# Score and projection matmuls on column tiles of 32, in a convolution-gate and attention kernel

## The chip, the cores and the metric

One NeuronCore of a Trainium2 chip runs the whole program in one launch. The metric is the device time of one execution in microseconds (us); the time before is the median of three runs.

## What is computed

`x` has 32 images of 64 channels and 16 x 16 pixels. The first layer gates it, the second is a group norm and an attention with 4 heads of 16 channels over the 256 pixels of an image.

```
y  = conv1d(mean(x, pixels), w_c);  yc = sigmoid(x * y)
sa = sigmoid(conv2d([mean_c(yc), max_c(yc)], w_s));  x1 = yc * sa + x
xn = groupnorm(x1, 32 groups) * gn_w + gn_b
q, k, v = split(qkv_w @ xn + qkv_b)         # 4 heads of 16
attn = softmax(q^T k / 4);  out = x1 + proj_w @ (attn v) + proj_b
```

## The kernel before

Two images make a pair, with the 64 channels of each on 64 of the 128 partitions; there are 16 pairs. A pair has 8 units, one for each image and head, and a unit has a score matrix of 256 x 256.

A unit's scores are computed twice. First `s(u)` (L663, matmul L670) makes q^T k into a bank of PSUM (the accumulator memory), and DVE takes the negated row maximum from it (L540). Then `st(u)` (L674, matmul L682) makes the transposed scores k^T q with one more contraction row, which holds that maximum, and ACT takes the exponential (L400). q and k are fp32 values split into bf16 parts; six products of parts are stacked into 96 contraction rows (`KQ`), so a score matmul is 96 or 97 rows by 128 columns of weights, with 256 moving columns, and a unit needs two of them for S and two for ST. Each has two banks, so `s(u)` waits for the reduction of unit u-2 (`max_done`) and `st(u)` for the exponential of unit u-2 (`exp_done`). `pv` (L686, matmul L696) multiplies the exponentials by v in fp32, each head on 32 columns of its own; an fp32 matmul runs as two passes, and each pass has a record of its own. `proj` (L718, matmul L726) is the output projection in fp32, on 64 columns for each image. `qk` (L707), `v` (L715) and `groupstats` (L734) are fp32 matmuls with 128 columns of weights. `maxt` (L741) transposes the maxima of a pair onto 16 rows.

The work is a pipeline of turns, its order written out by hand for each engine. Turn k does S of pair k+1, ST of pair k (its second half of slots) and of pair k-1 (its first half), PV of pair k-1 and the projection of pair k-2. A turn has 8 slots u. PE's order in it is: S, ST, maxt, qk(1) | S, ST, v | S, ST, pv | S, ST, pv | S, ST, proj | S, ST, pv | S, ST, pv | S, ST, groupstats, qk(0). Turns 2 to 9 are a loop of two laps with four turns in its body; the others are written out. Turns -1 and 0 also have `keep_busy` matmuls (L586), which do no work for the result.

The split parts of q and k go to HBM and come back stacked: SP writes `parts_dram` (L263), and one turn later reads it with six transfers (L255 and L256) into `qs` and `ks` for pair k+2. On SP's queue these six stand behind the transfer of the maxima of pair k (L243), which waits for ACT's copy `maxrow` (L388) of `maxt`'s result:

```
wait(sp, mrow_ready, k + 1)
sp.dma_start(qs[KQ:KQ + 1, slot(0), ...], maxrow[:, slot(0), :]).then_inc(mrow_in, 16)
...
wait(sp, parts_out, 16 * (k + 3))
```

The first S of a turn waits for all six (`stack_in`).

Of the kernel before, what the change touches and what calls it, by code (L numbers as in the profile page):

```python
# [22 lines left out]
P = 128  # L23
IMAGES, C, SIDE = 32, 64, 16
N = SIDE * SIDE
# [7 lines left out]
KQ = SLOTS * HD  # L33
# [18 lines left out]
def program(nc, x, w_rows, vecs, w_all, select, consts, out):  # L52
    ctx = ExitStack()
    with ctx:
        def sb(name, shape, dt=F32):
            return ctx.enter_context(nc.sbuf_tensor(name, shape, dt))
# [46 lines left out]
        qs = sb("qs", [P, RING, HEADS, 2, N], BF16)  # L103
        ks = sb("ks", [P, RING, HEADS, 2, N], BF16)
# [9 lines left out]
        onorm = sb("onorm", [P, 2 * N])  # L114
# [5 lines left out]
        w_p = wall[:, 384:448]  # L120
# [3 lines left out]
        s_bank = [bank[0], bank[1]]  # L124
        st_bank = [bank[2], bank[3]]
# [4 lines left out]
        y_psum = bank[7][:, 0:256]  # L130
# [34 lines left out]
        def wait(eng, semaphore, value):  # L165

            if not isinstance(value, int) or value > 0:
                eng.wait_ge(semaphore, value)
# [12 lines left out]
        def stands_in(aside, k, u):  # L181

            if isinstance(k, int) and (k, u) in aside:
                aside[k, u]()
# [397 lines left out]
        def _(pe):  # L582
# [70 lines left out]
            for a in range(2):  # L653
                mm = pe.matmul(bank[5][64 * a:64 * a + 64, 0:1], w_p, b_v, start=True, stop=True)
# [7 lines left out]
            def turn(k, slot, has, lap):  # L662
                def s(u):  # L663

                    a, h = u // HEADS, u % HEADS
                    wait(pe, max_done, UNITS * (k + 1) + u - 1)
                    if u == 0:
                        wait(pe, stack_in[slot(1)], lap(1) * 96)
                    for t in range(TILES):
                        mm = pe.matmul(s_bank[u % 2][:, t * N:(t + 1) * N], qs[0:KQ, slot(1), h, a, t * P:(t + 1) * P],  # L670
                                       ks[0:KQ, slot(1), h, a, :], start=True, stop=True)
                    mm.then_inc(s_ready, 1)

                def st(u):  # L674

                    d, unit = (-1, u + LEAD) if u < LEAD else (0, u - LEAD)
                    a, h = unit // HEADS, unit % HEADS
                    wait(pe, exp_done, UNITS * k + u - LEAD - 1)
                    if unit == 0:
                        wait(pe, mrow_in, 16 * (k + 1))  # L680
                    for t in range(TILES):
                        mm = pe.matmul(st_bank[u % 2][:, t * N:(t + 1) * N], ks[0:KQ + 1, slot(d), h, a, t * P:(t + 1) * P],  # L682
                                       qs[0:KQ + 1, slot(d), h, a, :], start=True, stop=True)
                    mm.then_inc(st_ready, 1)

                def pv(a, t):  # L686

                    if t == 0:
                        wait(pe, exp_done, UNITS * (k - 1) + HEADS * (a + 1))
                        if a == 1 and isinstance(k, int) and k == PAIRS:  # L690
                            pe.wait_ge(norm_step, 4 * (k - 1) + 1)
                        if a == 0:
                            wait(pe, norm_step, 4 * (k - 2) + 1)
                            wait(pe, vs_ready, k)
                    for h in range(HEADS):
                        mm = pe.matmul(o_bank[32 * h:32 * h + 32, a * N:(a + 1) * N], vs[:, slot(-1), t, a, h, :],  # L696
                                       pt[:, HEADS * a + h, t, :], start=(t == 0), stop=(t == TILES - 1))
                    if t == TILES - 1:
                        mm.then_inc(pv_done, 1)

                def qk(a):

                    d = 4 - a
                    if a == 0:
                        wait(pe, xn_ready, k + 5)
                        wait(pe, z32_ready, k + 4)
                    mm = pe.matmul(z_bank[:, a * N:(a + 1) * N], w_qk[a], xn[:, slot(d), :], start=True, stop=True)  # L707
                    if a == 1:
                        mm.then_inc(z_ready, 1)

                def v():

                    wait(pe, mrow_ready, k + 1)
                    for t in range(TILES):
                        mm = pe.matmul(v_psum[:, t * P:(t + 1) * P], xn[:, slot(1), t * P:(t + 1) * P], w_v, start=True, stop=True)  # L715
                    mm.then_inc(v_ready, 1)

                def proj():  # L718

                    wait(pe, norm_step, 4 * PAIRS + 4 if isinstance(k, int) and k == PAIRS + 1 else 4 * (k - 1))  # L720
                    if has(4):
                        wait(pe, gn_var, k + 5)
                    else:
                        wait(pe, yo_ready, k - 2)
                    for a in range(2):
                        mm = pe.matmul(y_psum[64 * a:64 * a + 64, :], w_p, onorm[:, a * N:(a + 1) * N], start=True, stop=True)  # L726
                    mm.then_inc(y_ready, 1)

                def groupstats():

                    wait(pe, gn_stat, 3 * (k + 6))
                    wait(pe, gn_var, k + 5)
                    wait(pe, yo_ready, k - 1)
                    mm = pe.matmul(gs_psum, groupavg, mv[:, :], start=True, stop=True)  # L734
                    mm.then_inc(gs_ready, 1)

                def maxt():

                    wait(pe, max_done, UNITS * (k + 1))
                    wait(pe, vs_ready, k + 1)  # L740
                    mm = pe.transpose(mt_psum, negmax[:, slot(0), :, :, :].rearrange("p h a t -> p (h a t)"), identb[:, :])  # L741
                    mm.then_inc(mt_ready, 1)

                for u in range(UNITS):
                    stands_in(aside, k, u)
                    if has(1):
                        s(u)
                    if has(-1 if u < LEAD else 0):
                        st(u)
                    if u == 0 and has(0):  # L750
                        maxt()
                    if u == 0 and has(3):
                        qk(1)
                    if u == 1 and has(1):
                        v()
                    if u in (2, 3) and has(-1):
                        pv(0, u - 2)
                    if u == 4 and has(-2):
                        proj()
                    if u in (5, 6) and has(-1):  # L760
                        pv(1, u - 5)
                    if u == 7 and has(5):
                        groupstats()
                    if u == 7 and has(4):
                        qk(0)
# [55 lines left out]
```

## Time and profile before

| what | value |
|---|---|
| median of 3 runs | 203.35 us (202.46 to 203.69) |
| span of the profiled execution | 198.1 us |
| PE busy | 175.1 us, 88%, 1422 matmul records |
| DVE busy | 150.4 us, 76% |
| ACT busy | 122.6 us, 62% |
| POOL busy | 106.3 us, 54% |
| chain that ended last | PE 55%, DMA 16%, SP's queue 12%, DVE 7% |

The profiled execution has no time of its own beside its span: the span runs from its first to its last instruction, and the runs' median lies 5.2 us above it. PE is TensorE's matmuls, PEld its weight loads, SPq SyncE's queue of transfers. Busy time overlaps between engines, so the shares don't add up to the span.

### The profile page before, as it was taken

How to read it: one execution, taken by the hardware profiler on the slowest of the kernel's cores; microseconds unless marked ns; L12 is line 12 of the kernel's file. 1: busy time of each engine (PE TensorE's matmuls, PEld its weight loads, DVE VectorE, ACT ScalarE, POOL GpSimd, SP SyncE). 2: the span in 40 equal slices, each digit the busy share in tenths (PEclk: the TensorE clock that was granted, in tenths of full speed). 3: DMA queues.
4: the chain of work that ended last, by engine and by line, in shares of the span. 5: the costliest groups of instructions: out<-in, count | busy, mean ns of one | idle time of the engine just before them, and what ended most of it. 6: DMA issues, size and time to landing. Idle time of an engine off the chain costs nothing.

```text
span 198.1 us, 4537 instructions
## 1 busy us (share of the span) xinstructions
PE 175.1 (88%) x1422; PEld 95.9 (48%) x1422; DVE 150.4 (76%) x327; ACT 122.6 (62%) x250; POOL 106.3 (54%) x181
## 2 busy tenths in 40 slices
PE   7579869796859899989999999999999998988981
PEld 2156557363535456454645556464655644453320
DVE  0867696477847898978889898988998779697263
ACT  3075323261538587858777787877868786666860
POOL 4991562665737476848595776759556360101110
PEclk9999996999999999999999999999999999999999
DMA  3930405599696663837474665847475573800001
GB/s 81 361 102 18 109 2 149 112 243 187 168 197 161 146 147 122 164 108 164 154 192 113 175 116 150 160 124 185 132 200 108 165 155 112 187 2 26 4 26 53
DMA packets 19558, 26.16 MB, mean 132 GB/s; under 512 B 3757, under 2 KB 16469, under 8 KB 19541
## 3 DMA queue, kind: packets, MB, share of 16 engines
q1 hardware_dynamic: 18960, 25.40, 51.9%
q10 hardware_dynamic: 580, 0.55, 1.2%
q8 instruction: 9, 0.15, 0.3%
q14 instruction: 9, 0.07, 0.1%
HBM read 17.29 MB, written 8.42 MB: 130 GB/s over the span
## 4 chain that ended last, share of the span: by engine, by line
PE 55%; DMA 16%; SPq 12%; DVE 7%; issue 4%; POOL 4%; ACT 1%; POOLq 0%; DVEq 0%
PE bank L696 14%; PE bank L670 12%; PE bank L682 10%; DMA ks<-parts_dram 8%; PE bank L707 7%; DMA parts_dram<-parts 6%; SPq L255 5%; SPq L256 4%; PE bank L726 4%; PE bank L715 2%; DMA con<-consts 2%; DVE maps L453 1%; PE bank L609 1%; POOL tapprod L289 1%; SPq L209 1%
## 5 line engine op out<-in xcount | busy, mean ns | idle before, releaser
L540 DVE TENSOR_REDUCE negmax<-bank 128x2 bf16<-128x512 f32 x128 | 86.9, 681 | 25.2 <-PE bank L670 24.8
L400 ACT ACTIVATE pt<-bank 128x512 f32<-128x512 f32 x128 | 75.4, 596 | 21.9 <-PE bank L682 21.7
L670 PE MATMUL bank<-ks,qs 96*128 96x256 bf16 x256 | 49.7, 275 | 7.4 <-DMA ks<-parts_dram 6.3
L682 PE MATMUL bank<-qs,ks 97*128 97x256 bf16 x256 | 48.8, 272 | 1.7 <-ACT pt L400 1.0
L696 PE MATMUL bank<-pt,vs 128*32 128x256 f32 x512 | 40.7, 391 | 0.1
L670 PEld LDWEIGHTS bank<-ks,qs 96*128 96x128 bf16 x256 | 18.4, 97 | 44.9 <-issue 26.4
L682 PEld LDWEIGHTS bank<-qs,ks 97*128 97x128 bf16 x256 | 23.9, 98 | 8.7 <-ACT pt L400 3.3
L339 POOL TENSOR_TENSOR xall<-yo,xall 128x256 f32 (+1 forms) x15 | 10.9, 729 | 26.8 <-ACT yo L420 26.8
L325 POOL TENSOR_TENSOR rest<-z,parts 128x512 f32<-128x512 f32 x15 | 17.4, 1158 | 14.2 <-ACT z L409 10.7
L707 PE MATMUL bank<-xn,wall 128*128 128x256 f32 x64 | 22.2, 436 | 0.0
L311 POOL TENSOR_TENSOR sq<-gmv 128x1 f32<-128x1 f32 x16 | 3.1, 193 | 34.4 <-DVE gmv L501 34.4
L586 PE MATMUL bank<-warm 128*128 128x512 bf16 x60 | 18.8, 427 | 1.4 <-POOL warm L280 1.4
L335 POOL TENSOR_TENSOR parts<-rest,parts 128x512 bf16<-128x512 f32 x15 | 17.4, 1157 | 1.3
L696 PEld LDWEIGHTS bank<-pt,vs 128*32 128x32 f32 x512 | 10.3, 108 | 13.7 <-issue 11.6
L392 ACT ACTIVATE xn<-xall,gnb,gna 128x256 f32<-128x256 f32 (+1 forms) x16 | 9.5, 592 | 11.6 <-DVE gnb L507 11.6
L521 DVE STREAM_TRANSPOSE otok<-bank 128x512 f32<-128x512 f32 (+1 forms) x17 | 11.5, 676 | 5.0 <-PE bank L696 5.0
L406 ACT ACTIVATE parts<-bank,vec 128x512 bf16<-128x512 f32 x16 | 10.9, 682 | 7.0 <-PE bank L707 7.0
L388 ACT COPY maxrow<-bank 16x128 bf16<-16x128 bf16 x16 | 4.1, 254 | 16.9 <-PE bank L741 16.9
L726 PE MATMUL bank<-onorm,wall 128*64 128x256 f32 x64 | 10.4, 405 | 1.6 <-DVE onorm L532 1.6
L532 DVE STREAM_TRANSPOSE onorm<-otok 128x512 f32<-128x512 f32 (+1 forms) x17 | 11.4, 673 | 0.1
L409 ACT ACTIVATE z<-bank,vec 128x512 f32<-128x512 f32 x16 | 11.0, 686 | 0.0
L707 PEld LDWEIGHTS bank<-xn,wall 128*128 128x128 f32 x64 | 10.3, 199 | 1.2
(67 smaller groups left out, 212.2 us busy)
## 6 DMA issues: line engine op xcount, KB each, us to landing
parts_dram<-parts SPq DMA_DIRECT2D x16, 384.0 KB, 2.7
qs<-parts_dram SPq DMA_DIRECT2D x16, 192.0 KB, 3.7
ks<-parts_dram SPq DMA_DIRECT2D x16, 192.0 KB, 3.9
xall<-x SPq DMA_DIRECT2D x4, 512.0 KB, 5.9
qs<-parts_dram SPq DMA_DIRECT2D x16, 128.0 KB, 3.8
ks<-parts_dram SPq DMA_DIRECT2D x16, 128.0 KB, 3.9
out<-xall SPq DMA_DIRECT2D x16, 128.0 KB, 2.1
gate<-gate_dram SPq DMA_DIRECT2D x6, 256.0 KB, 4.2
```

Source lines behind the costliest of these rows:

```text
L325: nc.gpsimd.tensor_tensor(rest[:, :], z32[:, :], parts[:, r, 0, :], ALU.subtract).then_inc(split_step, 1)
L335: nc.gpsimd.tensor_tensor(parts[:, r, 2, :], rest[:, :], parts[:, r, 1, :], ALU.subtract).then_inc(split_step, 1)
L400: nc.scalar.activation(pt[:, (u + LEAD) % UNITS, :, :].rearrange("p t n -> p (t n)"), st_bank[u % 2][:, :], ACT.Exp, scale=SCALE).then_inc ...
L521: op = nc.vector.transpose(o_tok[:, blocks, :].rearrange("p b c -> p (b c)"), o_bank[:, cols])
L532: op = nc.vector.transpose(onorm[:, cols], o_tok[:, blocks, :].rearrange("p b c -> p (b c)"))
L540: nc.vector.tensor_reduce(negmax[:, slot(1), u % HEADS, u // HEADS, :], s_bank[u % 2][:, :].rearrange("p (t n) -> p t n", t=TILES), AX.X, ...
L586: pe.matmul(bank[:, :], warm[:, 0:P], warm[:, :], start=True, stop=True)
L670: mm = pe.matmul(s_bank[u % 2][:, t * N:(t + 1) * N], qs[0:KQ, slot(1), h, a, t * P:(t + 1) * P], ks[0:KQ, slot(1), h, a, :], start=True, ...
L682: mm = pe.matmul(st_bank[u % 2][:, t * N:(t + 1) * N], ks[0:KQ + 1, slot(d), h, a, t * P:(t + 1) * P], qs[0:KQ + 1, slot(d), h, a, :], sta ...
L696: mm = pe.matmul(o_bank[32 * h:32 * h + 32, a * N:(a + 1) * N], vs[:, slot(-1), t, a, h, :], pt[:, HEADS * a + h, t, :], start=(t == 0), s ...
L707: mm = pe.matmul(z_bank[:, a * N:(a + 1) * N], w_qk[a], xn[:, slot(d), :], start=True, stop=True)
L726: mm = pe.matmul(y_psum[64 * a:64 * a + 64, :], w_p, onorm[:, a * N:(a + 1) * N], start=True, stop=True)
```

## The change

Each S and each ST matmul of 128 columns of weights becomes four matmuls of 32 columns, written to the partitions 0, 32, 64 and 96 of the same bank, with the same 256 moving columns. Each projection matmul of 64 columns becomes two of 32. The semaphores stay: the last matmul of a unit increments as before.

```
-                        mm = pe.matmul(s_bank[u % 2][:, t * N:(t + 1) * N], qs[0:KQ, slot(1), h, a, t * P:(t + 1) * P],
-                                       ks[0:KQ, slot(1), h, a, :], start=True, stop=True)
+                        for j in range(0, P, 32):
+                            mm = pe.matmul(s_bank[u % 2][j:j + 32, t * N:(t + 1) * N],
+                                           qs[0:KQ, slot(1), h, a, t * P + j:t * P + j + 32],
+                                           ks[0:KQ, slot(1), h, a, :], start=True, stop=True)
...
-                        mm = pe.matmul(st_bank[u % 2][:, t * N:(t + 1) * N], ks[0:KQ + 1, slot(d), h, a, t * P:(t + 1) * P],
-                                       qs[0:KQ + 1, slot(d), h, a, :], start=True, stop=True)
+                        for j in range(0, P, 32):
+                            mm = pe.matmul(st_bank[u % 2][j:j + 32, t * N:(t + 1) * N],
+                                           ks[0:KQ + 1, slot(d), h, a, t * P + j:t * P + j + 32],
+                                           qs[0:KQ + 1, slot(d), h, a, :], start=True, stop=True)
...
-                        mm = pe.matmul(y_psum[64 * a:64 * a + 64, :], w_p, onorm[:, a * N:(a + 1) * N], start=True, stop=True)
+                        for j in range(0, C, 32):
+                            mm = pe.matmul(y_psum[C * a + j:C * a + j + 32, :], w_p[:, j:j + 32], onorm[:, a * N:(a + 1) * N],
+                                           start=True, stop=True)
```

## Rows read from the trace of the kernel before

**Rows 1.** The page: busy time, the instruction queue, the transfer of maxima.

```profile
PE 175.1 (88%) x1422; PEld 95.9 (48%) x1422; DVE 150.4 (76%) x327; ACT 122.6 (62%) x250; POOL 106.3 (54%) x181
...
q8 instruction: 9, 0.15, 0.3%
...
qs<-maxrow SPq DMA_DIRECT2D x16, 4.0 KB, 1.7
```

**Rows 2.** Busy time by stretch, one turn of the loop.

```profile
104.50:113.30 8.80, 8.80 (x81) 4.91 (x80) 7.71 (x19) 6.86 (x14) 6.30 (x11) 1.00 0.60 149
```

**Rows 3.** Chain that ended last, from one maxt to the next.

```profile
104.53 0.15 PE bank L741
...
105.31 0.22 PE bank L670 x2
...
106.64 0.57 PE bank L696 x8
107.20 0.33 PE bank L670 x2
...
108.86 0.58 PE bank L726 x4
...
113.31 0.15 PE bank L741
```

**Rows 4.** Timeline of PE: start, length, line, operands, count.

```profile
104.15 0.38 PE L682 MATMUL bank<-qs,ks 97*128 97x256 bf16 x2
104.46 0.22 PE L741 MATMUL bank<-identb,negmax 128*16 128x128 bf16 x1
104.61 0.70 PE L707 MATMUL bank<-xn,wall 128*128 128x256 f32 x2
...
105.37 0.38 PE L682 MATMUL bank<-qs,ks 97*128 97x256 bf16 x2
105.59 0.61 PE L715 MATMUL bank<-wall,xn 128*128 128x128 f32 x4
```

**Rows 5.** Timeline of the weight loads, with idle time before them, two places.

```profile
101.13 0.16 PEld L696 LDWEIGHTS bank<-pt,vs 128*32 128x32 f32 x8 [0.21 <-issue]
...
192.31 0.15 PEld L696 LDWEIGHTS bank<-pt,vs 128*32 128x32 f32 x4
...
192.53 0.16 PEld L696 LDWEIGHTS bank<-pt,vs 128*32 128x32 f32 x4
```

**Rows 6.** Groups by line and shape: count, busy us, mean ns, idle before.

```profile
L682 PEld LDWEIGHTS bank<-qs,ks 97*128 97x128 bf16 x256 | 23.9, 98 | 8.7 <-ACT pt L400 3.3 <-issue 1.6 <-DMA qs<-maxrow 0.8
...
L696 PEld LDWEIGHTS bank<-pt,vs 128*32 128x32 f32 x512 | 10.3, 108 | 13.7 <-issue 11.6 <-ACT pt L400 2.0
...
L741 PEld LDWEIGHTS bank<-identb,negmax 128*16 128x16 bf16 x16 | 1.4, 85 | 3.8 <-issue 3.2 <-DVE negmax L540 0.6
```

**Rows 7.** Timeline of SP's queue, first and last transfer of a turn's seven.

```profile
105.00 0.54 SPq L243 DMA_DIRECT2D qs<-maxrow  x1
...
108.82 0.42 SPq L256 DMA_DIRECT2D ks<-parts_dram  x1
```

**Rows 8.** Landing of the ks transfer issued at 108.82; first S after it.

```profile
DMA to landing us min/median/max: 3.3/3.3/3.3
```

**Rows 9.** Timeline of PE at the first S of that turn.

```profile
112.71 0.27 PE L670 MATMUL bank<-ks,qs 96*128 96x256 bf16 x1
```

**Rows 10.** Chain that ended last, two turns that a transfer ended.

```profile
161.70 3.67 DMA ks<-parts_dram
165.51 0.38 PE bank L670 x2
...
174.08 0.38 PE bank L670 x2
```

**Rows 11.** Chain that ended last, the last two turns.

```profile
181.72 0.70 DVE negmax L540
...
188.93 0.60 ACT pt L400
```

## The prediction

> **What bounds the kernel now.** I read the page first: PE is busy for 88% of the span, DVE for 76% [rows 1]. That says little about a stage, so next the chain of waits. Up to 67.8 us it runs over the parts transfers and SP's queue. From there to 157 us nearly every piece is PE's: a turn goes from one maxt to the next in 8.78 us [rows 3], PE is busy for all of it, DVE for 7.71, ACT for 6.86, POOL for 6.30 [rows 2]. From 157 to 174 it runs over maxrow, SP's queue and the landing of ks to the first S [rows 10]. The last 24 us are PE with DVE's norm at the end.
>
> Within the turn the reader is to see that the same two matmuls cost differently by what stands before them. Two S after qk or v take 0.22 us, after a PV group 0.33 [rows 3]. The timeline shows why: weight loads of a PV group start after 0.21 us of idle time that nothing in the profile explains [rows 5]; maxt starts 0.31 after a pair of ST where v, which also follows ST, starts 0.22 after it [rows 4]. What differs is the number of weight columns: 128 against 32, 64 or 16. Between fp32 and bf16, and between 96 and 97 rows, nothing is lost. So PE loses about 0.1 us at each change of the column tile, and there are twelve in a turn: into and out of four PV groups and the projection, into and out of maxt.
>
> **A second bound lies right behind PE.** Turn k's six stack transfers stand behind the maxima on SP's queue, and the maxima need maxt of the same turn. From maxrow's transfer to the issue of the last ks is 3.82 us [rows 7], and it lands 3.3 later [rows 8], at 112.1. The first S of the next turn starts at 112.71 [rows 9]. An S that waits for the landing starts 0.14 after it (161.70 + 3.67, then 165.51 [rows 10]), so this turn had 0.46 us to spare. I went through the twelve turns from the S at 67.85 to the one at 174.08 in the same way (the last ks issue, its landing, the S): the landing took 3.3 to 4.25, and the spare time is 0.11, 0, 0.20, 0.46, 0.46, 0, 0.05, 0.10, 0.01, 0.09, 0 and 0, in all 1.5 us. In the transfer's own turns the period from S to S is 8.57 (165.51 to 174.08 [rows 10]).
>
> **The change part by part.**
>
> *S and ST.* A matmul of 128 columns becomes four of 32, so a unit's four matmuls become sixteen. What has to be known is how long four such matmuls take together. PV is made of them: eight weight loads and their matmuls fit in 0.57 us with the drains [rows 3], and within a long PV stretch four loads start every 0.22 us (192.31, 192.53 [rows 5]), which is the two passes' 0.44 of an fp32 matmul of 256 columns, no more than one alone would need. So four tiles run beside each other at full rate in fp32. In bf16 one needs 0.11 us (two S in 0.22). The limit is then the weight load, which must be hidden under 0.11 us: it takes 98 ns for 128 columns in bf16 now, 108 ns for 32 in fp32, 85 ns for 16 in bf16 [rows 6]. 32 columns in bf16 aren't in the trace; between its neighbours it is 85 to 108 ns, and I take 98. Bounds of a group of four: 0.11 (hidden) and 0.15 (after a drain the second loads of PV start 0.03 late; 0.03 + 0.11 + 0.01). I take 0.11, since inside a stream the loads start with the matmuls.
>
> The Trainium skill (TensorEngine Tiling, Restrictions) says that column tiling switches the fast weight load off, which speaks against the change. By it each small load costs as much as the large one did; the trace's 108 ns for 32 columns against 98 for 128 agrees, and the sum is the same as long as the four loads run beside each other, as PV's do.
>
> *Changes of tile that go.* All in one turn. Four PV groups: 0.57 becomes 0.44, and the S after it 0.33 becomes 0.22 [rows 3]: 4 x 0.24 = 0.96. Projection: 0.58 becomes 0.44, and 0.11 at the S: 0.25. Into maxt: 0.09 (0.31 against 0.22 [rows 4]).
>
> *Changes of tile that come.* qk, v and groupstats keep 128 columns and now stand between matmuls of 32. Out of qk(1), qk(0) and v: 0.10 each (maxt to qk is 0.15 [rows 4] where its 128 moving columns need 0.05). Into v and into groupstats: 0.20 each, 0.10 for the drain and 0.10 because their weight load, 0.11 from one to the next, no longer runs under ST. Into qk(1) from maxt: as now. Together 0.70.
>
> PE's turn: 8.78 - 0.96 - 0.25 - 0.09 + 0.70 = 8.18 us, 0.60 less. The Trainium skill (TensorEngine Tiling, Key Properties) has the rule that a change of tiling mode drains the engine; without this rule the sum would be 0, with it 0.60, and the 0.21 of idle time [rows 5] agree with it.
>
> *What is late next.* DVE needs 7.7 in a turn, ACT 6.9; slot by slot DVE falls at most 0.35 us behind (unit 2's reduction, two norm steps) and two banks cover it. The transfer chain does bind. It becomes shorter only by maxt's 0.09, since S to maxt is part of it: 8.57 becomes 8.48, and where a landing took 3.3 us, 8.25, just above PE's 8.18. So the twelve turns give the spare 1.5 us and 12 x 0.09 = 1.1: 2.6 us, not 12 x 0.60 = 7.2. PE will stand idle for some 0.3 us a turn before the first S.
>
> *The end.* From 174.08 no stack transfer is waited for. Turn 14 (S, ST, PV, proj, v): 4 x 0.24 + 0.25 + 0.09 + 0.15 (maxt to S) - 0.30 = 1.15, which ends at the last reduction, 181.72 [rows 11]. In the next turn five excursions of 0.24 go, but ACT's exponentials of 0.6 become its bound, so about 1.0 up to the exponential at 188.93 [rows 11]. The last PV stretch gives 0.4; the norm and the last projection are DVE's chain and stay. Together 2.5.
>
> *Turns before 67.8.* Turns -1 and 0 get new changes of tile around keep_busy, some 0.2 a slot. PE waits there for transfers of 3 to 5 us; without that cover it would be 3 us.
>
> *Instructions.* 96 pairs of weight load and matmul more for S and ST and 4 for the projection in each turn, beside 79 now. PE's code is what the instruction queue carries, 0.15 MB [rows 1], and it about doubles; the body of the loop with it. A jump back to code that has to be fetched again would cost up to one small transfer, 1.7 us [rows 1], once. Bounds 0 and 2 us (no gain is possible from more code), I take 0.6.
>
> **Sum.** 2.6 + 2.5 - 0.6 = 4.5 us: span 198.1 to 193.6, and 203.35 to 198.9 with the same 5.2 us around it.
>
> **Rivals.**
> 1. *The groups cost more than 0.11 and eat the gain.* PE's turn is 8.18 + 32 x (g - 0.11), 32 groups a turn. At g = 0.13 it is 8.8, as now: nothing in the loop, nothing at the end, 0.6 for the fetch: about 203. For it: no row has a bf16 load of 32 columns, and 108 + 10 ns would already be 0.12. Chance 0.15.
> 2. *Slower: the weight loads of the four tiles aren't hidden.* The place is every S and ST group; it decides from g = 0.13 on. At g = 0.15, PV's pattern behind a drain, PE's turn is 9.5 and the twelve turns lose 0.7 each, the last two 1.3: 203.35 + 8.4 + 1.3 - 0.5 = 212. Against it: in the long PV stretch no such gap is seen [rows 5]. Chance 0.12.
> 3. *Issue.* If PE's sequencer spent 62 ns on a matmul, a group would take 0.25, a turn 12.7, and the time would be about 250. The eight loads of PV that start within 0.16 us [rows 5] speak against it, though they may have been queued. Chance 0.03. It is the rule of the Trainium skill (TensorE: Matmul & The Clock Gate, Part 1) for one of two decode settings; the other, 25 ns a matmul, would leave 0.11 as it is.
> 4. *The transfers don't bind.* If landings came at 3.3 each turn, as in three of the twelve, PE's full 0.60 would count in most turns: 5.5 + 2.5 - 0.6 = 7.4, 196. Landing times depend on the chip's other traffic, which the change doesn't touch. Chance 0.07.
> 5. *The change doesn't do what it says*, since the idle time hangs on something else than the tile (the start of fp32 with own columns): PE's turn stays, or adds drains: 203 to 205. Chance 0.04.
>
> **How the numbers follow.** The forecast, 198.9, has 0.59: between 197.5 (no fetch, a little more at the end) and 200.9 (2 us of fetch). A measurement of this kernel tells about 1% from no change, 201.3 to 205.4. Faster: 0.59 + 0.07 + a part of rival 1 that still gains, 0.03 = 0.69. Within 1%: the other 0.12 of rival 1 and rival 5, 0.16. Slower: rivals 2 and 3, 0.15. The range takes in the forecast, rival 4 and rival 1: 195.8 to 204.5; rivals 2 and 3 and part of rival 5, 0.17, lie outside.
>
> **What the profile after would show.** Four S or ST matmuls starting within some 0.03 us, the next four 0.11 later: the first step; 0.13 or more: rivals 1 and 2. A PV group directly behind ST with no idle time of the weight load before it, and S after it in 0.22. New idle time of 0.2 before v and before groupstats. A turn from S to S of 8.3 to 8.7 with PE idle before the first S and released by the ks transfer: the second bound. DVE's reductions waiting less for S. The jump back near 103 us with or without a gap in PE. I would be wrong by most if PE's sequencer were the new bound, which would show as gaps inside a group while both semaphores had long been given.

## The result, and the profile after

The changed kernel takes 206.75 us (median of 4 runs, 206.4 to 207.28) against 203.52 us of the kernel before on the same chip (4 runs, 202.46 to 203.81): ratio 1.0187, 95% interval 1.0143 to 1.0231. The forecast was faster, 198.9 in a range of 195.8 to 204.5. Both sign and range missed. Ratios leave out runs that lie more than 1.5% above the fastest of their kernel, so a ratio isn't always that of the medians beside it (of m1's six runs below, one of 202.8 us and one of 232.37 us with a granted clock of 0.66 are left out).

The spans of the profiled executions lie further apart than the times: 205.5 against 198.1. The time of the changed kernel's profiled execution was 207.28, that is 1.8 us above its span, and every later run kept this distance. So the profiled execution of before took about 199.9 us, less than any of the four measured ones, and there are not 5.2 us of surroundings beside its 198.1.

The page after, the lines that answer to [rows 1], and the groups that answer to [rows 6] with the one of `gnb` (count, busy us, mean ns, idle before):

```profile
PE 176.3 (86%) x3022; PEld 108.8 (53%) x3022; DVE 158.2 (77%) x327; ACT 123.5 (60%) x250; POOL 106.6 (52%) x181
...
q8 instruction: 18, 0.29, 0.7%
```

```profile
L671 PEld LDWEIGHTS bank<-ks,qs 96*32 96x32 bf16 x1024 | 21.9, 97 | 48.0 <-issue 17.0 <-DVE negmax L540 16.1 <-DMA ks<-parts_dram 1.9
L700 PEld LDWEIGHTS bank<-pt,vs 128*32 128x32 f32 x512 | 15.3, 114 | 1.6 <-ACT pt L400 0.7
L507 DVE SCALAR_TENSOR_TENSOR gnb<-gmv,gna,vec 128x1 f32<-128x1 f32 x16 | 11.4, 713 | 5.1 <-POOL gna L331 5.0
```

A load of 32 columns in bf16 takes 97 ns for S (99 for ST), as forecast (98). PV's idle time before the load went from 13.7 us to 1.6: the changes of tile are gone there. New is a wait of S for DVE's reduction, 16.1 us in all. DVE is busy for 8 us more although its work is the same 327 instructions: 4.8 of these are `gnb` (L507), an addition on 128 x 1 values, 713 ns on average where it took 412. Another 4.0 are `mv` (L492), also on 128 x 1 values: 0.78 us in most turns of the loop where it took 0.25, beside POOL's L305 (0.72 us). Nothing is late by it: `groupstats`, which waits for `mv`, starts 0.33 us after the last ST whether `mv` took 0.20 or 0.78.

One turn of the loop, the windows view (answers to [rows 2]; the second row is a stretch at a granted clock of 0.5):

```profile
118.20:127.30 9.10, 8.54 (x180) 5.50 (x179) 8.81 (x18) 6.97 (x14) 6.31 (x11) 1.00 0.56 145
88.10:94.80 6.70, 6.70 (x80) 3.85 (x75) 3.89 (x9) 3.69 (x8) 3.62 (x8) 0.50 0.60 119
```

PE is busy for 8.54 of 9.10 us, DVE for 8.81. The chain that ended last through the same turn (answers to [rows 3]):

```profile
120.06 0.64 PE bank L719 x4
120.70 0.36 PE bank L671 x8
...
122.32 0.58 DVE negmax L540
...
123.81 1.08 DVE gnb L507
...
125.51 0.58 ACT pt L400
...
126.14 0.40 PE bank L685 x8
126.54 0.31 PE bank L740 x2
126.85 0.54 PE bank L711 x2
127.39 0.33 PE bank L671 x8
```

The reader is to see three parts. From the first S to the S of slot 2 the chain is PE's, over both new changes of tile, out of `qk` and around `v`. From 121.1 to 126.1 it runs over DVE's queue, `gnb`, then ACT's `xn` and an exponential, down to the last ST: PV and projection, where the removed changes of tile were, lie beside it. From the last ST to the next first S it is PE again, over `groupstats` and `qk(0)`, 1.25 us. The turn lasts 9.11.

The timeline of PE at slots 2 and 3 (answers to [rows 4]), and that of the weight loads (answers to [rows 5]):

```profile
121.08 0.61 PE L700 MATMUL bank<-pt,vs 128*32 128x256 f32 x8
...
121.95 0.61 PE L700 MATMUL bank<-pt,vs 128*32 128x256 f32 x8
```

```profile
119.99 0.52 PEld L719 LDWEIGHTS bank<-wall,xn 128*128 128x128 f32 x4 [0.21 <-issue]
```

A PV slot takes 121.95 - 121.08 = 0.87 us: 0.43 for PV, 0.22 for S, 0.22 for ST, with nothing between. A group of four matmuls of 32 columns takes 0.11. Before `v` the weight load stands idle for 0.21. All of this is as forecast, and so is PE's own work in a turn: 3.00 us up to slot 2's ST, five times 0.87, and 0.85 for `groupstats` and `qk(0)` make 8.2.

Next come the first stack transfer on SP's queue (0.56 us in [rows 7]'s turn and in most others) and the landing of the last ks, in a turn that holds a fetch of PE's code (answers to [rows 7, 8]). The fetch is the row of the instruction queue in the stretch from 100.6 to 109.3:

```profile
100.67 1.38 SPq L255 DMA_DIRECT2D qs<-parts_dram  x1
```

```profile
q8 instruction: 1, 0.02, 1.1%
```

```profile
DMA to landing us min/median/max: 4.4/4.4/4.4
```

From `maxrow` to the issue of the last ks this turn takes 4.9 us and the landing 4.4; the turn lasts 10.06. In the four turns behind it, without a fetch, it is 4.1 to 4.2 and 3.2 to 3.6, and the turns last 9.11 to 9.13.

Where the 7.4 us between the two spans are: the first `maxrow` comes at 49.3 and 49.2; the fifteen turns from there to the last `maxrow` took 133.4 us before and 142.4 after (+9.0); from the last `maxrow` to the end it is 15.4 and 13.9 (-1.5).

### The profile page after: what moved, and what is told of

The parts are those of the page before. It is cut to its first block, busy times and chain, and to the rows that moved or that the text cites. A ratio compares the mean times of both kernels' runs of the same rounds, so it can differ in the third digit from the quotient of the medians.

```text
span 205.5 us, 7737 instructions
## 1 busy us (share of the span) xinstructions
PE 176.3 (86%) x3022; PEld 108.8 (53%) x3022; DVE 158.2 (77%) x327; ACT 123.5 (60%) x250; POOL 106.6 (52%) x181
## 4 chain that ended last, share of the span: by engine, by line
PE 31%; DMA 21%; SPq 16%; DVE 15%; issue 8%; ACT 4%; POOL 3%; DVEq 0%; ACTq 0%; POOLq 0%
DMA ks<-parts_dram 12%; SPq L255 8%; DMA parts_dram<-parts 7%; PE bank L671 7%; PE bank L685 6%; PE bank L711 6%; SPq L256 5%; PE bank L700 4%; DVE negmax L540 3%; DVE gnb L507 3%; PE bank L719 3%; ACT pt L400 3%; DMA con<-consts 2%; PE bank L740 1%; DVE maps L453 1%
## 5 line engine op out<-in xcount | busy, mean ns | idle before, releaser
L540 DVE TENSOR_REDUCE negmax<-bank 128x2 bf16<-128x512 f32 x128 | 85.6, 678 | 26.9 <-PE bank L671 25.2
L400 ACT ACTIVATE pt<-bank 128x512 f32<-128x512 f32 x128 | 73.9, 591 | 15.4 <-PE bank L685 14.6
L671 PE MATMUL bank<-ks,qs 96*32 96x256 bf16 x1024 | 52.5, 282 | 13.5 <-DMA ks<-parts_dram 9.9
L685 PE MATMUL bank<-qs,ks 97*32 97x256 bf16 x1024 | 52.1, 281 | 2.0 <-ACT pt L400 0.8
L671 PEld LDWEIGHTS bank<-ks,qs 96*32 96x32 bf16 x1024 | 21.9, 97 | 48.0 <-issue 17.0
L685 PEld LDWEIGHTS bank<-qs,ks 97*32 97x32 bf16 x1024 | 26.3, 99 | 9.3 <-ACT pt L400 6.7
L711 PE MATMUL bank<-xn,wall 128*128 128x256 f32 x64 | 23.0, 449 | 0.0
L335 POOL TENSOR_TENSOR parts<-rest,parts 128x512 bf16<-128x512 f32 x15 | 17.5, 1164 | 1.3
L388 ACT COPY maxrow<-bank 16x128 bf16<-16x128 bf16 x16 | 4.1, 254 | 23.2 <-PE bank L747 23.2
L700 PEld LDWEIGHTS bank<-pt,vs 128*32 128x32 f32 x512 | 15.3, 114 | 1.6 <-ACT pt L400 0.7
L507 DVE SCALAR_TENSOR_TENSOR gnb<-gmv,gna,vec 128x1 f32<-128x1 f32 x16 | 11.4, 713 | 5.1 <-POOL gna L331 5.0
L719 PE MATMUL bank<-wall,xn 128*128 128x128 f32 x64 | 12.8, 328 | 0.0
```

Source lines behind the costliest of these rows:

```text
L335: nc.gpsimd.tensor_tensor(parts[:, r, 2, :], rest[:, :], parts[:, r, 1, :], ALU.subtract).then_inc(split_step, 1)
L400: nc.scalar.activation(pt[:, (u + LEAD) % UNITS, :, :].rearrange("p t n -> p (t n)"), st_bank[u % 2][:, :], ACT.Exp, scale=SCALE).then_inc ...
L507: nc.vector.scalar_tensor_tensor(gnb[:, :], gmv[:, 0:1], gna[:, 0:1], b_gn, ALU.mult, ALU.add).then_inc(gn_shift, 1)
L540: nc.vector.tensor_reduce(negmax[:, slot(1), u % HEADS, u // HEADS, :], s_bank[u % 2][:, :].rearrange("p (t n) -> p t n", t=TILES), AX.X, ...
L671: mm = pe.matmul(s_bank[u % 2][j:j + 32, t * N:(t + 1) * N], qs[0:KQ, slot(1), h, a, t * P + j:t * P + j + 32], ks[0:KQ, slot(1), h, a, :] ...
L685: mm = pe.matmul(st_bank[u % 2][j:j + 32, t * N:(t + 1) * N], ks[0:KQ + 1, slot(d), h, a, t * P + j:t * P + j + 32], qs[0:KQ + 1, slot(d), ...
```

## The experiments

Each kernel is compared with the kernel before on the same chip, in the same batch. The theories: **collision** (DVE's `gnb` now starts beside a subtraction on POOL and is held by it), **changes of tile** at the wrong places, **code** (more fetches, which lengthen the transfer chain), **clock** (a granted clock of 0.5 more often).

**e1: gnb earlier, in the changed kernel.**

```
+                    if u == 4:
+                        if has(5):
+                            wait(dve, gn_stat, 3 * (k + 5) + 1)
+                        if has(4):
+                            gn_shifts()
                     if has(1):
                         wait(dve, s_ready, UNITS * (k + 1) + u + 1)
```

(`gn_shifts`, which writes `gnb`, is taken out of its place behind unit 4's reduction.)

> The changed kernel with one step moved on DVE: the group norm's shift (gnb, L507) ahead of the reduction of unit 4 instead of behind it. Theory 1 (a collision of DVE and POOL): in the loop turns of the changed kernel gnb takes 1.07 us because it starts 0.12 us after POOL's subtraction of the third part (L335, 1.16 us) and ends only with it; before, it took 0.21 and ended before that subtraction began. Moved ahead by a reduction (0.6 us), it should take 0.21 again, the turn from first S to first S should fall from 9.12 to about 8.5 to 8.65 (the transfer chain), and the median from 206.75 to about 202 to 204. Theory 2 (the low clock between 88 and 95 us and at 184 us makes the loss): gnb gets short, the loop turns get shorter, but the low windows stay and the median falls by less than 1 us. Theory 3 (the tile changes cost more than 0.1 us each): no change beyond 0.5 us.

Measured: 202.94 (12 runs, 200.4 to 205.69), ratio 1.0056 [0.9987, 1.0126]. `gnb` takes 0.28 us in most turns. In the turns without a fetch the period is 8.54 to 8.93 (but for one of 9.91, which holds 3.4 us at a granted clock of 0.5), and the chain is now the transfers':

```profile
122.65 3.88 DMA ks<-parts_dram
...
126.66 0.40 PE bank L672 x8
```

The collision costs 1.3% by these ratios (1.0187 to 1.0056) and 2.2% by the second measurement of the changed kernel (r1, 1.0276); the two kernels were not measured side by side. Behind it stands the bound that the prediction named. Turns with a fetch last 8.8 to 10.3.

**e2: the same edit in the kernel before.**

> Control: the kernel before with the same step moved. In seven of its eight loop turns gnb takes 0.21 us already, and PE and the transfers bound the turn. Theory 1: within 0.5% of the kernel before (203.5), perhaps 0.5 us faster by the one late turn in which gnb took 1.20. If the move by itself brings as much here as in the changed kernel, the collision isn't what the change caused.

Measured: 201.53, ratio 1.0014 [0.9967, 1.006]; turns of 8.79 as without it. The edit by itself gives nothing where PE is the bound.

**e3: S in 128 columns, ST and projection on tiles of 32**, so that tiles change sixteen times a turn.

```
-                        for j in range(0, P, 32):
-                            mm = pe.matmul(s_bank[u % 2][j:j + 32, t * N:(t + 1) * N], ...
+                        mm = pe.matmul(s_bank[u % 2][:, t * N:(t + 1) * N], qs[0:KQ, slot(1), h, a, t * P:(t + 1) * P],
```

> The changed kernel with S back on 128 columns and ST and the projection on 32: every slot of a turn now changes the tile from S to ST and back, 16 changes in a turn against 12 before and 6 in the changed kernel. If a change costs about 0.1 us whatever the neighbours, PE's turn is 8.2 + 10 x 0.1 = 9.2 to 9.3, all of it PE, and the time about 203.5 + 0.45 x 10 + 1 = 207 to 210. If a change costs nothing between S and ST (both bf16), PE's turn is 8.4 and the time about 204.

Measured: 203.05 (202.23 to 204.33), ratio 1.0131 [0.9989, 1.0274]. The loop's turns last 9.28, all PE's:

```profile
118.45 0.22 PE bank L670 x2
118.67 0.33 PE bank L683 x8
119.00 0.43 PE bank L698 x8
119.43 0.32 PE bank L670 x2
```

S after a PV group on tiles costs 0.32 where it costs 0.22 behind `v`, and so does ST after S, 0.33: 0.1 a change, in bf16 too. The term of the sum holds. Here too `gnb` takes 1.1 us, and it delays nobody: PE's chain is longer. The time was lower than expected: two late turns took 8.59, and from the last `maxrow` to the end it is 13.9 us as in the changed kernel, not 15.4. The turns of 9.28 keep PE busy throughout, and no stretch at a granted clock of 0.5 falls among them.

**e4: all on tiles of 32**, `qk`, `v` and `groupstats` too, no change of tile but the two of `maxt`.

```
-                    mm = pe.matmul(z_bank[:, a * N:(a + 1) * N], w_qk[a], xn[:, slot(d), :], start=True, stop=True)
+                    for j in range(0, P, 32):
+                        mm = pe.matmul(z_bank[j:j + 32, a * N:(a + 1) * N], w_qk[a][:, j:j + 32], xn[:, slot(d), :], start=True, stop=True)
```

(`v` and `groupstats` in the same way.)

> The changed kernel with qk, v and groupstats on column tiles of 32 as well, so that a loop turn has no change of tile. PE's turn should be 8.2 - 0.7 = 7.5 us. v no longer delays S of slot 2 by 0.29, so DVE reaches gnb about 0.3 us earlier, ahead of POOL's subtraction. Theory 1: gnb takes 0.21, the turn falls from 9.12 to about 8.5 (transfer chain), median about 201 to 203. Theory 2: PE idles even more, so the clock falls at least as often, and the median stays at 206 or above. Theory 3: all its price is gone here, median below 203.

Measured: 208.17 (206.91 to 210.71), ratio 1.0366 [1.0243, 1.0489], the slowest of the small edits, though PE has least to do. The jump back to the loop's first turn in the chain, the instruction queue, and the branch of PE's sequencer (min/median/max of its two executions in ns):

```profile
102.70 3.83 DMA ks<-parts_dram
106.53 2.49 issue
109.02 0.40 PE bank L671 x8
```

```profile
q8 instruction: 30, 0.49, 1.0%
...
L194 PEldq COMPARE_BRANCH  x2: 83/2392/4701, 104.0 to 144.9; - x2
```

PE stood for 4.45 us before that S, 2.49 of them after the landing and with nothing to wait for but the branch, which took 4.70 us; in the changed kernel it took 0.25 and there is no such gap. In the second lap PE's code is fetched again, eight times from 106.3 to 139.3 us, where the changed kernel has no fetch between 106.3 and 150.1 (9, 18 and 30 fetches in all in before, changed and this). The turns take 8.9 to 9.9 but for the 12.03 of the jump; eight of the twelve from the third `maxrow` on end on a landing. So in this kernel the size of the code costs: the loop's body no longer stays loaded.

**r1: the changed kernel again.**

> The changed kernel once more, unchanged, so that the others of this call can be compared with it on the same chip and in the same hour. If the first measurement holds, it is 1.5 to 2.5% above the kernel before, and about 1 to 1.5% above what the moved gnb gave (ratio 1.006).

Measured: 208.1 (205.25 to 210.88), ratio 1.0276 [1.0207, 1.0346], with the same turns of 9.11 to 9.14 and `gnb` of 1.07. Both measurements of the changed kernel together say 2 to 3% slower.

**e5 and e6: the maxima on ACT's queue**, in e1's kernel and in the kernel before, so that no stack transfer stands behind them.

```
                         nc.scalar.copy(maxrow[:, slot(0), :], mt_psum).then_inc(mrow_ready, 1)
+                        wait(act, mrow_ready, k + 1)
+                        act.dma_start(qs[KQ:KQ + 1, slot(0), ...], maxrow[:, slot(0), :]).then_inc(mrow_in, 16)
```

(SP waits for `exp_done` at UNITS * (k - 1) in place of `mrow_ready`.)

> The changed kernel with gnb ahead of unit 4's reduction and with the transfer of the maxima on ACT's queue instead of SP's, so that the six stack transfers no longer wait for maxt (they wait for the exponentials of the turn before instead). Theory A (a second bound: first S, maxt, maxrow, SP's queue, landing): the loop turns of the run with gnb early took 8.54 to 8.98 us with S 0.14 us behind the landing; freed of it they should go to PE's own 8.2 to 8.3, and turns with late landings (9.6 to 9.9) lose their excess too; together 0.4 to 1.0 us a turn, 4 to 8 us, time about 196 to 199. Theory B (after the collision is gone DVE or PE bound the turn): no more than 1 us faster than the run with gnb early.

> Control: the kernel before with the maxima on ACT's queue. Theory A: only the turns that ended on a landing get shorter (71 to 87 us, 157 to 175 us), the others are PE's 8.79 and stay: 1 to 2.5 us faster, 0.5 to 1.2%. If it gains as much as the same step in the changed kernel, the transfer chain hid nothing of the change's gain.

Measured: e5 202.1, ratio 1.0017 [0.9961, 1.0073]; e6 206.14, ratio 1.0203 [1.0141, 1.0264]. In e5 the last ks lands 0.5 us or more before the first S in most turns, and still the turns last 9.1. Its chain has found another way round:

```profile
106.86 0.53 ACTq L387
...
109.26 0.59 ACT z L409
...
112.01 0.69 DVE negmax L545
...
112.74 0.40 PE bank L672 x8
```

The issue of the transfer takes 0.53 us of ACT's time, ahead of `z`; POOL's subtraction and `gna` follow later, and DVE, with `gnb` at the head of its queue, holds the reductions back. In e6 the maxima land late in an early turn, since stack transfers are no longer held behind them, and ST waits:

```profile
69.96 4.99 DMA qs<-maxrow
...
75.00 0.39 PE bank L682 x2
```

My expectation of a gain in both was wrong: the transfer chain was freed, but its cost moved to ACT.

**e7: the changed kernel, turns 2 to 9 written out.**

```
-            with eng.Fori(0, (LOOP_TO - LOOP_FROM) // RING, 1) as laps:
...
+            peeled(range(-AHEAD, PAIRS + BEHIND))
```

> The changed kernel with turns 2 to 9 written out instead of the loop of two laps: the work and its order stay, but PE's code of four turns (about 1500 instructions) is fetched once more in place of being run again. Theory C (PE's code fetches delay the stack transfers, in SP's issue by about 0.7 us and in the landing by about 0.8): turns 6 to 9, which took 9.12 us without a fetch, now hold fetches and end on landings, 9.4 to 10 us; 1 to 3 us slower than the changed kernel. Theory D (the fetches are harmless): same time, perhaps 0.3 us faster since the jump is gone.

Measured: 204.83, ratio 1.0168 [1.0123, 1.0213], no slower than with the loop (1.0276 in the same batch), with 24 fetches instead of 18. `gnb` takes 0.9 us in it instead of 1.07, so the edit changes more than the code. That more fetches alone make a kernel slower is not borne out here, and not refuted.

**e8 to e11: a square.** e8 has e1's edit and no loop; e10 is the kernel before without the loop; e9 and e11 are these two with four of the six stack transfers ahead of the maxima on SP's queue.

```
+                    if not isinstance(k, int) or k >= 2:
+                        wait(sp, exp_done, UNITS * (k - 1))
                     wait(sp, parts_out, 16 * (k + 3))
...
+                        if first == 5 and has(0):
+                            maxima()
```

> The changed kernel with both repairs met so far: the group norm's subtraction gnb ahead of unit 4's reduction on DVE, and the turns 2 to 9 written out instead of looped (more fetches of PE's code, lighter waits). It is the control for the next kernel. The first bound (transfer chain) and the collision are the two causes held so far: with the collision gone and the loop gone, turns without a fetch of PE's code should last 8.5 to 8.7 and end on the landing of ks (first S 0.14 after it), turns with a fetch 9.2 to 9.6. Span 199 to 201, time 201 to 203. If the loop's heavier waits had no part in it: as the run with gnb early alone, 202.9.

> As the kernel before it, and on SP's queue four of a turn's six stack transfers now stand ahead of the maxima and two behind them, so the last ks is issued some 2 us earlier and no longer waits for maxrow. Theory C (the transfer chain, lengthened by fetches of PE's code, is what keeps the changed kernel from PE's 8.18 us): landing 1 us or more before the first S in nearly all turns, turns without a fetch 8.2 to 8.4, with one 8.3 to 8.6, twelve turns 5 to 8 us shorter than in the control, time 195 to 198: faster than the kernel before. Rival D (a cycle over ACT, POOL and DVE stands right behind, as in the run with the maxima on ACT's queue): the landing is early but turns stay at 8.6 to 9.1 with PE waiting for DVE or ACT; time within 1% of the control. Rival E (the clock): turns are short, but the granted clock falls as often as now, 1 to 3 us of the gain are lost: 197 to 200.

> The kernel before, turns 2 to 9 written out: the control for the next one. PE is the bound with 8.78 us a turn; the body of the loop was fetched once and kept, now some 5 fetches of PE's code more. If fetches cost what they cost in the changed kernel (landing later by 1 us in such a turn, where 0.46 us or less are spare) : 2 us slower, 204 to 206. If the lighter waits make up for it, as in the changed kernel without the loop: within 0.5%, 201 to 203.

> The kernel before without the loop, four stack transfers ahead of the maxima. Theory C: the landing no longer ends any turn, the turns in which it did (0.11 us or less to spare in 7 of twelve) become 8.78: 1 to 2.5 us less than the control. If this gains as much as the same edit in the changed kernel (3% or more), the transfers were worth more than PE's turn in both and theory C sees too small a part of it.

Measured: e8 202.95, ratio 1.0059 [1.0011, 1.0107], all its turns ending on the landing, 8.61 to 9.41 us in the twelve from the third `maxrow` on but for one of 10.39; e9 224.61, ratio 1.1099 [1.103, 1.1167]; e10 201.57, ratio 0.9998 [0.9948, 1.0047]; e11 227.31, ratio 1.121 [1.1135, 1.1285]. The order on SP's queue failed in both in the same way, by a cycle that I had overlooked. Its chain in e9:

```profile
103.15 2.54 DMA parts_dram<-parts
...
109.13 3.12 DMA qs<-maxrow
```

The stack transfers wait for the parts to land in HBM, the maxima behind them, ST behind the maxima, the exponentials and `z` behind ST, the parts behind `z`. e9 and e11 say nothing on theory C.

e10 holds something else. Without the loop the kernel before has the collision too: POOL's subtraction starts 5.39 us after the first S instead of 5.57, nine of the sixteen `gnb` take 1.2 us, and the turns are none the longer for it:

```profile
129.00 1.21 DVE L502 SCALAR_TENSOR_TENSOR gnb<-gmv,gna,vec 128x1 f32<-128x1 f32 x1
```

```profile
122.82 0.22 PE bank L677 x2
123.04 0.12 PE bank L729 x2
123.16 0.54 PE bank L702 x2
123.70 0.32 PE bank L665 x2
```

Five of its twelve turns last 8.79, with 1.2 us of `gnb` in them, and none of the others is tied to it. The kernel before has one such turn with its loop as well, from the S at 139.16: 1.20 us of `gnb`, 8.79 us. From the last ST to the next first S it needs 0.88 us where the changed kernel needs 1.25 (0.18 more for an ST that had to wait, 0.19 more around `groupstats`). So the collision alone doesn't make 9.11; it needs PE's own stretches to be longer. This opened the last question.

**m1 to m3: the tiles of 32 only where they help.** In m1 S and ST are on tiles of 32 in the slots 2 to 6, beside PV and the projection, and on 128 columns in the slots 0, 1 and 7. m2 is m1 with e1's edit. m3 has 128 columns in slot 7 alone.

```
+                    w = 32 if 2 <= u <= 6 else P
                     for t in range(TILES):
-                        for j in range(0, P, 32):
+                        for j in range(0, P, w):
```

> The changed kernel, but S and ST are on tiles of 32 only in the slots 2 to 6, where PV and the projection stand; in the slots 0, 1 and 7, beside qk, v and groupstats, they are single matmuls of 128 columns again. Four changes of tile a turn are left (v to S, PV to the S of slot 7, and the two around maxt), where the kernel before has twelve and the changed one seven. PE alone needs 8.78 - 0.85 (four PV groups, one exit stays) - 0.25 (projection) + 0.10 (v to S) = 7.8. The norm on DVE stays late, gnb may take 1.1 again. Theory F (the new changes of tile around v, groupstats and qk(0) lie in the stretch that only PE sets, those removed lie beside DVE's chain): the collision stays, but the chain over it needs about 6.6 (first S to gnb's end) + 1.2 (xn and exponentials to the last ST) + 0.9 (last ST to the next first S) = 8.7; turns without a fetch 8.6 to 8.7. Rival G (the collision alone makes the turn long): 9.0 to 9.1 as in the changed kernel, time 204 or more. Code grows by 64 pairs a turn instead of 100. Time by theory F 200 to 203.

> As the kernel before it, with gnb ahead of unit 4's reduction. No collision; by theory F only the transfer chain is left, turns 8.55 to 8.6 ending 0.14 after the landing, 0.1 less than without this edit: time 0.5 to 1 us less than the kernel before it, 199.5 to 202, level with or 1% below the unchanged kernel. Rival G: 9.1 falls to 8.6, 4 us or more less than without.

> The changed kernel with S and ST of 128 columns in slot 7 alone: the changes of tile into groupstats and out of qk(0) move to the S of slot 7 (beside DVE's chain) and to v's side they stay. Theory F: last ST to the next first S becomes 0.9 to 1.0 instead of 1.18, the turn of 9.11 becomes 8.8 to 8.9; time 1 to 2 us less than the changed kernel. Rival G: 9.1 stays.

Measured: m1 199.66, ratio 0.9886 [0.9806, 0.9966]; m2 198.24, ratio 0.9885 [0.9818, 0.9952]; m3 204.96, ratio 1.0195 [1.0118, 1.0272]. Both m1 and m2 are faster than the kernel before by about 1.1%. In m1 a turn ends on the landing:

```profile
118.34 3.66 DMA ks<-parts_dram
...
122.14 0.38 PE bank L672 x2
```

`gnb` takes 0.20 us in the whole loop of m1, without e1's edit: the S of slot 2 starts 2.22 us after the first S (113.31 and 115.53), not 2.42 (118.21 and 120.63), the norm on DVE keeps its place, and `gnb` is through before POOL's subtraction starts. So m2 has nothing left to remove. It also means that m1 doesn't test theory F as it was meant to, with the collision in place: in m1 the collision is gone as well. m3 keeps the collision, and its turn is 8.97:

```profile
112.30 1.09 DVE gnb L507
...
114.64 0.39 PE bank L687 x2
115.04 0.17 PE bank L742 x2
115.20 0.54 PE bank L713 x2
115.74 0.33 PE bank L672 x8
```

From the last ST to the first S it takes 1.10 instead of 1.25, and the turn is shorter by just that, 0.15 (expected 0.2 to 0.3). That the turn follows this stretch one for one shows that it lies in the cycle. By the time of the whole m3 gains nothing that can be told from the changed kernel. What speaks for theory F is the length of the steady turn here and, against G, the turns of e10, which have the collision and last 8.79.

## Why the prediction was wrong

**The steps that held.** The group of four takes 0.11 us and its loads 97 to 99 ns, so rivals 1, 2 and 3 fell. PV behind ST loses nothing; S to `maxt` is shorter by 0.08, where 0.09 was forecast (first S to `maxrow` 0.79 before, 0.71 after). The price of a change of tile, 0.1, held in the changed kernel and in e3, and the new ones stand where they were forecast. The Trainium skill (TensorEngine Tiling, Key Properties) has the drain at a change of mode; this case's size for it is 0.1 us. The transfer chain is the bound that was named: where nothing else is in the way (e1, e8, m1) turns end 0.14 after the landing, at 8.54 to 8.93 in e1's turns without a fetch, against a forecast of 8.48.

**The step that failed: "What is late next".** It said that DVE "falls at most 0.35 us behind" and "two banks cover it", and that only the transfer chain binds. The sum of PE's turn, 8.18, was right, but it took every change of tile as equal. They aren't. The ten that go (around PV and the projection) lie in slots 2 to 6, beside DVE's reductions, norm and `gnb`; the ones that come lie around `v`, `groupstats` and `qk`, in the stretches that only PE can fill. Slot 2's S starts 0.31 later after the first S (2.42 for 2.11), DVE's five instructions up to `gnb` run without a gap, and `gnb` starts at 5.60 after the first S instead of 5.37. POOL's subtraction (L335, 1.16 us) starts at 5.48 there. Before, `gnb` was ahead of it and took 0.21; now it is behind and takes 1.07, to 0.03 after POOL's end. The same two instructions, before and after:

```profile
109.29 0.21 DVE L507 SCALAR_TENSOR_TENSOR gnb<-gmv,gna,vec 128x1 f32<-128x1 f32 x1
...
109.50 1.16 POOL L335 TENSOR_TENSOR parts<-rest,parts 128x512 bf16<-128x512 f32 x1
```

```profile
123.81 1.07 DVE L507 SCALAR_TENSOR_TENSOR gnb<-gmv,gna,vec 128x1 f32<-128x1 f32 x1
...
123.69 1.16 POOL L335 TENSOR_TENSOR parts<-rest,parts 128x512 bf16<-128x512 f32 x1
```

This was in the trace of before: `gnb` ended at 109.50, where POOL's subtraction began. I had not looked at the two together. The Trainium skill (SBUF — State Buffer, Who interferes with whom) says that a DVE instruction with two inputs in SBUF contends with a GpSimd instruction that reads SBUF, that the port pair they share is an exclusive lock, and that the order of issue decides which of the two waits. The rows agree: 0.21 alone, 1.07 behind a POOL instruction of 1.16 us that began 0.12 earlier. The recorded starts tell the order only roughly, though: in e10 `gnb` is recorded 0.03 us ahead of POOL's subtraction and still takes 1.21, to 0.02 after its end.

The turn of 9.11 is then: 6.67 (first S to `gnb`'s end) + 1.26 (`xn` and an exponential, to the last ST) + 1.18 (start to start, to the next first S). In the kernel before without its loop the same three need 6.57, about 1.17 (an estimate: the least that the changed kernel's trace shows) and 0.88 (1.06 with what an ST adds after a wait), in all 8.6 to 8.8. That is level with PE's 8.79 at most, and so it is hidden; measured there are 6.57, 1.34 and 0.88, since PE's own chain is the longer one. e1 takes the collision away (8.54 to 8.93), m3 shortens the third part (8.97), m1 the first (no collision, 8.69 to 8.81 in the loop's turns but for one of 8.36).

**The second step that failed: "Instructions".** It priced the code by a single fetch at the jump back, 0.6 us. The jump back costs nothing (the branch takes 0.24 us before and 0.25 after), but fetches of 16 KB stand beside the transfers in most turns outside the loop's second lap: 18 in all, for 9. In the ten traces of kernels with the new tiles and this order of transfers (the changed kernel, r1, e1, e3, e4, e7, e8, m1 to m3) the twelve turns from the third `maxrow` on were gone through: from `maxrow` to the landing of the last ks it takes 7.69 us on average in the 28 turns without a fetch and 8.24 in the 92 with one. In three traces of the kernel before and its variants (before, e2, e10) it is 7.67 in 16 turns and 7.94 in 20. So a fetch goes with 0.3 to 0.5 us more where the landing is what ends the turn. e4 speaks for the code as cause. But no kernel changed the code alone, nearly all the turns without a fetch lie in the loop's second lap, and in e7 more fetches did not make the kernel slower. So this part stays argued.

**The rivals.** The slower case was given 0.15, all of it to costs inside the groups and of PE's issue. The one that came, DVE's chain by way of POOL, was none of them. Rivals 4 and 5 didn't come either.

**The clock.** In the changed kernel PE ran at a granted clock of 0.5 from 88.1 to 94.8 us (1.2 GHz in place of 2.4), after a stretch in which PE had been busy for 2.8 of 4.1 us, and that turn lasted 11.13; r1 shows the same at 89.4, with 10.79. The kernel before had no such stretch there; its variants e6 and e10 had one at other places. A turn of this kind costs about 1 us more than its neighbours with a fetch. It follows PE's idle time in these traces; nothing was run to separate it. The sum had no term for it.

**The end.** Forecast 2.5 less; from the last `maxrow` on it was 1.5 less (15.4 to 13.9), but the turn ahead of it, 7.86 before, was 8.43. That turn holds a second stretch at a granted clock of 0.5, from 183.6 to 187.0, in which `v` took 1.12 us instead of 0.64. In e7, which has the same matmuls in this turn, the clock stayed full and the turn took 6.81. The windows of this turn in the changed kernel and in e7:

```profile
183.20:191.60 8.40, 8.05 (x169) 5.31 (x161) 6.51 (x12) 5.34 (x11) 0.74 (x1) 0.80 0.06 18
```

```profile
181.30:188.10 6.80, 6.45 (x173) 4.50 (x161) 6.28 (x12) 5.33 (x12) 0.73 (x1) 1.00 0.07 22
```

At full clock turn and end together are shorter by 2.5 us (23.2 before, 20.8 in e7), as forecast; the stretch at a granted clock of 0.5 takes 1.6 of them back. r1 has it in the same turn, also with 8.43.

**The base.** "With the same 5.2 us around it" was wrong too: 1.8 us lie around a span. The trace of before was that of an execution some 3.4 us faster than the median, and its granted clock was 0.99, where later executions of the same kernel had 0.94 to 0.99. This didn't change the sign.

**Shares, by ratios.** 1.0187 (1.0276 in the second batch) for the changed kernel; 1.0056 without the collision; 0.9885 with the changes of tile around `v`, `qk` and `groupstats` gone as well and 15 fetches for 18. The second step mixes tiles and code, and all of these ratios hold what the clock takes; these runs don't part them.

## What to carry to other kernels

A cost that goes and a cost that comes on the same engine don't cancel by their sum: put each into the stretch between two handovers, and ask which engine's chain sets that stretch. Here the same tiles placed only in slots 2 to 6 made 1.1% faster what they made 2 to 3% slower everywhere. When an engine is to be sped up by some tenths, look in the trace for pairs of VectorE and GpSimd instructions that miss each other by less than that; and know the span's distance to the time from a run that has both, before a sum is set on it.

## What was unexpected of the hardware

- An addition on 128 x 1 values on DVE takes 0.21 us alone and up to 1.21 us beside a POOL subtraction of 128 x 512, and ends 0.02 us after it.
- Matmuls on four column tiles start within 0.01 us of each other, and the next four 0.11 later, with loads of 97 to 99 ns hidden: for bf16 loads of 32 columns nothing was lost against those of 128.
- PE's code came in pieces of 16 KB; with 30 of them the branch back to the loop's head took 4.70 us, with 18 or 15 it took 0.25.
- A transfer of 4 KB landed after 1.7 us [rows 1] when the large ones stood behind it on its queue, and after 4.99 when they were already under way (e6).
